# Last stage: products with 128 stationary columns issued as two matmuls of 64 columns, one into each half of the partitions

## What is computed

```
xn = layernorm(x)
s  = attention(xn, W_qkv, W_proj, b_proj, gamma, beta, centers)     # 16 heads of 16
for l in range(2):                                                  # 8 heads of 64, windows of 128
    h = shift(x);  q, k, v = split(h @ wqkv)                        # 256 -> 3 * 512
    q, k = rotary(l2norm(q) * qs, l2norm(k) * ks)
    x = x + local_attention(q, k, v) @ wo                           # 512 -> 256
    h = layernorm(shift(x)) * lg + lb
    a, g = split(h @ w1 + b1)                                       # 256 -> 2 * 682
    x = x + (a * gelu(g)) @ w2 + b2                                 # 682 -> 256
out = x0 + s * silu(x)
```

## The kernel before

| line | work | tile | issued matmuls | TensorE instructions |
|---|---|---|---|---|
| L1622 | transpose the exponentials | 64x128, two row halves | 32 | 32 |
| L1555 | keys of item k+1 (n = 1), 512 moving columns | 128x128 | 2 | 4 |
| L1632 | transpose the inverse row sums | 128x128 | 4 | 4 |
| L1645 | attention times values | 128x64, two column halves | 16 | 32 |
| L1555 | queries of item k+1 (n = 0) | 128x128 | 2 | 4 |
| L1657 | product with wo | 128x128 | 8 | 16 |
| L1587, L1578, L1667 | transpose keys, queries, residual | 128x128 | 4, 4, 2 | 4, 4, 2 |
| L1566 | values of item k+1, 512 moving columns | 128x128 | 2 | 4 |
| L1606, L1678, L1606 | scores; transpose the normed rows; scores | 64x128 | 4, 4, 4 | 8, 4, 8 |
| L1690 | product with w1 (two of the 22 have 106 columns) | 128x128 | 22 | 44 |
| L1703 | product with w2 | 128x128 | 12 | 24 |
| L1713 | final items: heads' projection, 256 moving columns | 128x128 | 2 | 4 |
| L1722 | final items: transpose y | 128x128 | 2 | 2 |

## Time and profile before

### The profile page before, as it was taken

One profiled execution on the slowest core, in us unless ns is written; L12 is line 12 of the kernel. 1 busy time (PEld: TensorE's weight loads), 2 busy tenths in 40 slices (PEclk: granted clock), 3 DMA queues, 4 the chain that ended last, 5 costly groups with the idle time before them and its releaser, 6 DMA issues.

```text
span 2960.1 us, 97183 instructions
## 1 busy us (share of the span) xinstructions
PE 2919.8 (99%) x38016; PEld 1971.1 (67%) x38016; DVE 2325.1 (79%) x4219; ACT 2271.1 (77%) x4379; POOL 1111.0 (38%) x1835
## 2 busy tenths in 40 slices
PE   8999999999999999999989999999999999999998
PEld 4455555555555555555567777778777777877786
DVE  8888888888888888888856776667676667767665
ACT  4599999999999999999956666666666666666664
POOL 5421221111112211221245455555456554555554
PEclk9899999999999999999999999999999999999999
DMA  6631111111111111111121101111011111011110
GB/s 231 212 116 38 49 47 45 40 49 48 43 44 49 49 41 46 49 49 38 43 64 44 32 30 33 40 43 40 28 36 30 44 43 34 28 35 38 44 41 5
DMA packets 157206, 152.14 MB, mean 51 GB/s; under 512 B 17794, under 2 KB 130946, under 8 KB 156930
## 3 DMA queue, kind: packets, MB, share of 16 engines
q1 hardware_dynamic: 156930, 148.15, 16.0%
HBM read 89.37 MB, written 58.72 MB: 50 GB/s over the span
## 4 chain that ended last, share of the span: by engine, by line
PE 95%; DVE 3%; issue 1%; ACT 1%; SPq 0%; DMA 0%; POOL 0%; DVEq 0%; POOLq 0%; ACTq 0%
PE banks L1488 15%; PE banks L1450 15%; PE banks L1505 15%; PE banks L1690 11%; PE banks L1555 8%; PE banks L1703 6%; PE banks L1606 4%; PE banks L1645 4%; PE banks L1657 4%; PE banks L1566 4%; PE banks L1622 2%; PE banks L1578 1%; PE banks L1632 1%; PE banks L1587 1%; PE banks L1713 1%
## 5 line engine op out<-in xcount | busy, mean ns | idle before, releaser
L1146 DVE TENSOR_REDUCE pair_max<-banks 128x1 f32<-128x1024 f32 x1024 | 1219.7, 1222 | 145.5 <-PE banks L1450 115.8
L917 ACT ACTIVATE probs<-banks 128x512 f32<-128x512 f32 x2048 | 1158.7, 598 | 64.0 <-PE banks L1488 4.1
L1488 PE MATMUL banks<-q_aug,k_aug 98*32 98x512 bf16 x8192 | 1143.6, 381 | 0.8 <-ACT probs L917 0.4
L1450 PE MATMUL banks<-k_aug,q_aug 96*32 96x512 bf16 x8192 | 819.4, 382 | 5.3 <-ACT v_all L884 3.3
L1505 PE MATMUL banks<-probs,v_cur 128*32 128x256 f32 x8192 | 796.8, 379 | 0.2
L1488 PEld LDWEIGHTS banks<-q_aug,k_aug 98*32 98x32 bf16 x8192 | 391.7, 95 | 197.1 <-ACT probs L917 5.4
L1505 PEld LDWEIGHTS banks<-probs,v_cur 128*32 128x32 f32 x8192 | 366.8, 111 | 166.5 <-ACT acc_sb L898 0.8
L646 POOL TENSOR_SCALAR row_max<-pair_max 128x1 f32<-128x1 f32 x508 | 132.1, 283 | 886.5 <-DVE pair_max L1146 886.5
L1450 PEld LDWEIGHTS banks<-k_aug,q_aug 96*32 96x32 bf16 x8192 | 310.1, 97 | 218.2 <-DVE pair_max L1146 11.6
L1690 PEld LDWEIGHTS banks<-hnT,w_sb 128*128 128x128 f32 (+1 forms) x2816 | 320.2, 191 | 25.1 <-ACT hnT L997 25.1
L1690 PE MATMUL banks<-hnT,w_sb 128*128 128x128 f32 (+1 forms) x2816 | 332.4, 278 | 0.9 <-ACT hnT L997 0.9
(11 more groups left out here) (146 smaller groups left out, 4093.4 us busy)
## 6 DMA issues: line engine op xcount, KB each, us to landing
acc_scratch<-acc_sb SPq DMA_DIRECT2D x128, 256.0 KB, 2.4
heads_win<-acc_scratch SPq DMA_DIRECT2D x512, 64.0 KB
q_aug<-q_parts SPq DMA_DIRECT2D x192, 64.0 KB, 2.2
k_aug<-k_parts SPq DMA_DIRECT2D x192, 64.0 KB, 2.2
q_parts<-parts SPq DMA_DIRECT2D x16, 384.0 KB, 3.1
k_parts<-parts SPq DMA_DIRECT2D x16, 384.0 KB, 4.0
x_in<-in_x SPq DMA_DIRECT2D x10, 512.0 KB, 4.7
xT_scratch<-xnT SPq DMA_DIRECT2D x8, 512.0 KB, 5.2
```

The lines of the kernel that those rows point to most:

```text
L917: nc.scalar.activation(probs[:, step % PRING, :], banks[:, ring(h, use), :], ACT.Exp, scale=SCALE).then_inc(prob_ready, 1)
L1146: nc.vector.tensor_reduce(pair_max[:, group % 2, q, half:half + 1], banks[:, 4 + 2 * (t % 2):6 + 2 * (t % 2), :], AX.XY, ALU.max).then_inc ...
L1450: last = nc.tensor.matmul(banks[m:m + CT, 4 + t % 4, :], q_aug[0:TERM_ROWS, b, q * P + m:q * P + m + CT], k_aug[0:TERM_ROWS, b, kq * BANK: ...
L1488: last = nc.tensor.matmul(banks[m:m + CT, ring(h, use), :], k_aug[0:AUG, b, kb * P + m:kb * P + m + CT], q_aug[0:AUG, b, qc * CHUNK:(qc + ...
```

## The change

A helper `in_halves` splits a product along its stationary columns into pieces of `COLS` = 64 and issues the pieces one after the other, each into its own partitions of the same bank. The moving operand is the same for both. It is used for the queries, the values, and the products with wo, w1, w2 and the heads' projection. The keys (n = 1), all transposes and the scores keep their form. Nothing else is changed.

```diff
+COLS = 64
...
+            def in_halves(out, stationary, moving, start, stop):
+
+                cols = stationary.shape[-1]
+                for first in range(0, cols, COLS):
+                    size = min(COLS, cols - first)
+                    last = nc.tensor.matmul(out[first:first + size], stationary[:, first:first + size], moving,
+                                            start=start, stop=stop)
+                return last
+
...
             def project(i, k, n):
...
-                    last = nc.tensor.matmul(banks[:, lanes(b) + n, :], xT[:, l, b, f, 1 - f:1 - f + WINDOW],
-                                            wqkv_sb[:, l, f, n * INNER:(n + 1) * INNER],
-                                            start=(f == 0), stop=(f == 1))
+                    out, tokens = banks[:, lanes(b) + n, :], xT[:, l, b, f, 1 - f:1 - f + WINDOW]
+                    weights = wqkv_sb[:, l, f, n * INNER:(n + 1) * INNER]
+                    if n == 1:
+                        last = nc.tensor.matmul(out, tokens, weights, start=(f == 0), stop=(f == 1))
+                    else:
+                        last = in_halves(out, tokens, weights, start=(f == 0), stop=(f == 1))
...
-                        last = nc.tensor.matmul(banks[:, lanes(b) + 1, f * P:(f + 1) * P],
-                                                wo_sb[:, l, j, f * P:(f + 1) * P], oT[:, b, j, :],
-                                                start=(j == 0), stop=(j == NPAIR - 1))
+                        last = in_halves(banks[:, lanes(b) + 1, f * P:(f + 1) * P],
+                                         wo_sb[:, l, j, f * P:(f + 1) * P], oT[:, b, j, :],
+                                         start=(j == 0), stop=(j == NPAIR - 1))
```

More of the change, by code:

```diff
@@ L1565, in project_v @@
                 for f in range(2):
-                    last = nc.tensor.matmul(banks[:, lanes(b) + 2, :], xT[:, l, b, f, 1 - f:1 - f + WINDOW],
-                                            wqkv_sb[:, l, f, 2 * INNER:], start=(f == 0), stop=(f == 1))
+                    last = in_halves(banks[:, lanes(b) + 2, :], xT[:, l, b, f, 1 - f:1 - f + WINDOW],
+                                     wqkv_sb[:, l, f, 2 * INNER:], start=(f == 0), stop=(f == 1))
                 last.then_inc(v_ready, 1)
@@ L1689, in hidden @@
                     for f in range(2):
-                        last = nc.tensor.matmul(
-                            banks[0:width, lanes(b) + bank, place_ * P:(place_ + 1) * P],
-                            w1_sb[:, l, f, c * P:c * P + width], hnT[:, b, f, :], start=(f == 0), stop=(f == 1))
+                        last = in_halves(banks[0:width, lanes(b) + bank, place_ * P:(place_ + 1) * P],
+                                         w1_sb[:, l, f, c * P:c * P + width], hnT[:, b, f, :],
+                                         start=(f == 0), stop=(f == 1))
                 last.then_inc(w1_done, 1)
@@ L1702, in project_hidden @@
                     for f in range(2):
-                        last = nc.tensor.matmul(banks[:, lanes(b), f * P:(f + 1) * P],
-                                                w2_sb[:, l, j, f * P:(f + 1) * P], uT[:, b, j, :],
-                                                start=(j == 0 and f == 0), stop=(j == HB - 1 and f == 1))
+                        last = in_halves(banks[:, lanes(b), f * P:(f + 1) * P],
+                                         w2_sb[:, l, j, f * P:(f + 1) * P], uT[:, b, j, :],
+                                         start=(j == 0 and f == 0), stop=(j == HB - 1 and f == 1))
                 last.then_inc(w2_done, 1)
@@ L1712, in project_heads @@
                 for f in range(2):
-                    last = nc.tensor.matmul(banks[:, lanes(b) + 3, 0:D], heads_T[:, b, f, :], wp_sb[:, f, :],
-                                            start=(f == 0), stop=(f == 1))
+                    last = in_halves(banks[:, lanes(b) + 3, 0:D], heads_T[:, b, f, :], wp_sb[:, f, :],
+                                     start=(f == 0), stop=(f == 1))
                 last.then_inc(proj_done, 1)
```

## The result

| | before | after |
|---|---|---|
| median | 2961.99 us (2961.83 to 2963.34, 4 runs) | 3078.14 us (3072.9 to 3081.16, 4 runs) |
| ratio | | 1.039 [1.0375, 1.0405] |
| profiled execution | 2960.1 us | 3076.0 us |
| mean granted TensorE clock | 0.994 | 0.978 |

What follows compares the result with a forecast made beforehand. PE was taken as the bound, busy 99% of the span. A gain of 0.11 us in each of 64 items made 7.0 us: 2960.1 - 7.0 + 1.9 = 2955.0 us; range 2947 to 2963 us.

Steps and rivals of the forecast that it cites:

- 1, queries behind L1645: Queries after L1645, already in 64-column form: no change of form any more, -0.20 us an item.
- 2 to 4, wo, change, waits: Product with wo -0.04, change of form before the keys' transposes +0.16, waits for DVE that go -0.12 us an item.
- 5, change before the values: Going into 64 columns before the values +0.14, leaving their pairs +0.01 us an item.
- 6, L1690: Product at L1690: second start earlier by 0.05, closer spacing worth 0.10; together -0.15 us an item.
- 7, L1703 in a final item: Product at L1703 in final items: most gain turns into waiting for the gate's third part; -0.02 us left.
- change before L1722: Final items, before L1722: change back to 128 columns +0.10, leaving the pairs +0.01 us.
- 512-column pairs: Queries and values: four pairs at 0.43 us each as now, full overlap assumed (bounds 0 to +0.03).
- the spacing of 0.109 us: Two 64-column instructions side by side take 0.109 us, 0.0025 less than one 128-column instruction; taken from L1645.
- the wait at L1622's second half: In items not final, PE waits about 0.14 us there for L973's exponentials, cutting the gain to 0.11 us.
- The change part by part: Section pricing the edit on PE per item; summed to -0.11 us in both final and other items.
- Slower: issue rate: Rival: four instructions a pair with loads, issued at 0.124 us a pair; +1.03 us an item, 3026 us; chance 0.02.
- something that isn't in the trace: Remainder among the slower cases, with no place or size given; chance 0.02.

Runs made afterwards that it cites:

- experiment 6: The changed kernel with TensorE's loop over the windows written out, so nothing is jumped back to: 2953.24 us, ratio 0.9973.
- 7: The kernel before with TensorE's loop over the windows written out and nothing else changed: 2961.2 us, ratio 0.9997.
- 1: The changed kernel with one added instruction at the loop's top hinting that its closing branch will be taken: 2965.81 us, ratio 1.0012.
- 11: The kernel before, loop body at a block's start, queries and wo in pairs in three of four items (1760 instructions): 2954.03 us, ratio 0.997.
- slot 200: The kernel before, its loop body moved to begin at instruction 200 of a 256-instruction block, touching 8 blocks: 3071.36 us, ratio 1.0359.
- slot 165: The kernel before, its loop body moved to begin at instruction 165 of a 256-instruction block, touching 8 blocks: 2971.69 us, ratio 1.0039.

## Why the prediction was wrong, by its own steps

The steps on the pairs held. The one row of before that they need beside the earlier trace rows, the first scores of that item:

```profile
2017.04 1.13 PE L1606 MATMUL banks<-kT,qT 64*128 64x256 f32 x8
```

Timeline of PE in the kernel after, a final item away from the jump:

```profile
2085.65 5.02 PE L1553 MATMUL banks<-hnT,w_sb 128*64 128x128 f32 x88
2090.51 2.82 PE L1553 MATMUL banks<-pT,w_sb 128*64 128x128 f32 x48
2093.16 1.03 PE L1553 MATMUL banks<-wp_sb,heads_T 128*64 128x256 f32 x8
2094.12 0.44 PE L1735 MATMUL banks<-ident,yT 128*128 128x128 f32 x2
2094.49 1.21 PE L1635 MATMUL banks<-ident,masked 64*128 64x64 f32 x32
...
2097.98 1.97 PE L1658 MATMUL banks<-pT,vw 128*64 128x128 f32 x32
2099.78 1.89 PE L1553 MATMUL banks<-wqkv_sb,xT 128*64 128x512 f32 x8
2101.50 1.92 PE L1553 MATMUL banks<-oT,wo_sb 128*64 128x128 f32 x32
2103.34 0.66 PE L1600 MATMUL banks<-ident,pT 128*128 128x128 f32 x4
...
2104.62 1.94 PE L1553 MATMUL banks<-wqkv_sb,xT 128*64 128x512 f32 x8
2106.49 1.13 PE L1619 MATMUL banks<-kT,qT 64*128 64x256 f32 x8
```

| step | predicted | measured, from start to start, against the earlier trace rows |
|---|---|---|
| 1, queries behind L1645 | -0.20 | L1645 to wo: 3.72 before, 3.52 after: -0.20 |
| 2 to 4, wo, change, waits | 0.00 | wo to the values: 3.01 and 3.12: +0.11 with the change before the values (0.10 predicted for its first part) |
| 5, change before the values | +0.15 in both parts | values to scores 1.82 and 1.87: +0.05, its second part |
| 6, L1690 | -0.15 | 5.00 and 4.86: -0.14 |
| 7, L1703 in a final item | -0.02 | 2.71 and 2.65: -0.06 |
| change before L1722 | +0.11 | 0.87 and 0.96: +0.09 |

512-column pairs overlap wholly (four in 1.72 us), and the spacing of 0.109 us holds through long runs. Behind items that are not final the wait at L1622's second half came back as predicted: 0.11 and 0.17 us in experiment 6 against 0.14. A final item without that wait at its start takes 22.98 us (predicted 23.02). The item that the prediction named for the 23.02, from 2005.00 on, begins with the wait, and its like takes 23.17: the sum was right and the example badly chosen. A window takes 89.7 us instead of 90.2 (experiment 6), so 0.12 us an item where 0.11 was forecast. Freed of the jumps, the change gives 2953.24 us, and 2955 was forecast. The only term that was mis-sized is L1703 in final items, whose wait for the gate's third part did not stay: 0.04 us in half the items, 1.3 us in all.

**The step that failed is the one that isn't there.** "The change part by part" priced time on TensorE, waits and orders, and counted what the edit does to the program's length at nothing. The rival *Slower: issue rate* came near: it counted four instructions a pair, and asked whether they can be issued fast enough. They can. It didn't ask where they are kept. The 0.02 given to "something that isn't in the trace" was not only too small, it was also misnamed: the trace of before showed the resource, in the DMA view, as a queue that is busy in the second stage (12 packets between 300 and 388 us) and silent in the third once the loop runs. That silence is a loop that fits, and a rival that asks how much longer it may grow could have rested on it. How little room there was only the experiments show: seven blocks, 1792 instructions, of which 1640 leave 152, and 752 more are five times that.

A habit of the working hid it too. Every bound was the nearest row of an item, and an item's rows are the same wherever it stands in the loop. What happens once in four items, at the jump, has no row in an item's timeline.

## What to carry to other kernels

Before an edit that adds instructions inside a hardware loop, count the engine's instructions in the body and the 256-instruction blocks that it touches, and look whether the instruction queue is silent in that stretch: if it is, the loop lives on the core, and the edit can throw it out. Here seven blocks were free and eight cost up to 109 us with not one instruction added; ways out were to write the loop out (7), a hint for the jump (0.9 us a jump left, 1), or an edit that stays inside (11). And a change of column form paid here where a neighbour already had the form: the values, between two lines of 128 columns, lost 6.9 us (6 against 12) where the others together gained 15.6.

## What the runs showed of the hardware

- A float32 product is four TensorE instructions in the program, and code is fetched in packets of 16 KB, one per 256 of them (9.1 and 6.3 packets a window for 2392 and 1640). A fetch takes 0.9 to 2.1 us (kernel after) and is hidden when the code goes straight on (2961.2 us written out against 2961.9).
- A jump back to code that is no longer there cost 8.9 us (kernel after) or 7.8 us (before at slot 200), far more than a fetch: one or two waits of 1.1 to 4.4 us, and the lower clock behind them, 1.4 us on the keys alone. In the first wait shown above no packet of the queue was under way after 2019.3 us, and TensorE went on at 2021.40; where these 2 us go is not shown. "Advanced Engine Details and Errata" of the Trainium skill, section ISA Cache, speaks of "Only 2 cache lines!"; on TensorE the runs here contradict it, for they kept at least seven, and at 12 of 14 jumps at slot 165 eight.
- The mean granted clock fell from 0.994 to 0.978 through stalls alone; it is a symptom here, and the hint, which left the pairs as they were, brought it back to 0.993.
- Semaphore increments in a row are not free padding: 90 an item, nine in a row, cost 1.3 us an item (24.39 against 23.13 us), and 18 or 19 in a row showed waits for "issue" at the products behind them (136.9 us at L1691 in 1260 us).
